# A graph layer and a routed feed-forward layer: one layer norm in place of two, self loops on GpSimd, groups handed over by tile, logits in two banks

## The reference

```python
def gnn(x, C2, A):                       # called with C2 = A = adj
    adj = (A + A.T) * 0.5
    adj = adj + eye(N)                   # the self loops
    dinv = where(deg > 0, sum(adj, 1) ** -0.5, 0)
    adj = dinv[:, None] * adj * dinv[None, :]
    return C2 @ adj @ x                  # computed as adj @ x = Z, then C2 @ Z = Y

x1 = x + gnn(layernorm(x), adj, adj)     # layernorm: (x - mean) / sqrt(var + 1e-5)
t = layernorm(x1)                        # first norm of x1
h = (t - mean(t)) / sqrt(var(t) + 1e-5) * gamma + beta    # second norm, inside the FFN
shared = silu(h @ q(sw1).T) @ q(sw2).T   # q: rows rounded to -1, 0, 1 times mean |w|
probs = softmax(h @ router_w.T); e = argmax(probs)        # 8 experts
out = x1 + shared + max(probs) * (silu(h @ q(w1[e]).T) @ q(w2[e]).T)
```

## Time and profile before

| | |
|---|---|
| median of 3 runs | 729.55 us (727.76 to 730.76) |
| the profiled execution | 729.79 us |
| its span, first to last instruction | 728.1 us |
| mean granted TensorE clock | 0.986 of full |
| busy: TensorE, its weight loads | 91%, 53% |
| busy: VectorE, ScalarE, GpSimd | 67%, 54%, 28% |
| DMA | 151.68 MB, 208 GB/s on average |

### The profile page before, as it was taken

How to read it: one execution, slowest core, us unless ns; L and a number is a source line. 1 busy time by engine, 2 the same in 40 slices (tenths; PEclk the granted TensorE clock), 3 DMA queues, 4 the chain that set the end, 5 groups by cost and what they waited for, 6 DMA issues and landing times.

```text
span 728.1 us, 16147 instructions
## 1 busy us (share of the span) xinstructions
PE 659.4 (91%) x5313; PEld 385.2 (53%) x5313; DVE 488.8 (67%) x1071; ACT 390.1 (54%) x726; POOL 202.4 (28%) x195
## 2 busy tenths in 40 slices
PE   0799998999998999999868788799999999999995
PEld 0344443444444554444424365477767676777763
DVE  4878966646674556589899868966775465555554
ACT  2667547859986765777547662223342233233331
POOL 2123310000000000077666606620020445344332
PEclk9999999999999999999998999999999999999999
DMA  8999942675887787667566785354248677677751
GB/s 350 416 420 417 417 172 58 193 185 144 228 243 243 256 271 269 234 207 226 173 240 215 226 228 147 92 164 105 86 59 203 147 211 186 179 191 176 174 148 34
DMA packets 107103, 151.68 MB, mean 208 GB/s; under 512 B 64286, under 2 KB 64286, under 8 KB 102944
## 3 DMA queue, kind: packets, MB, share of 16 engines
q1 hardware_dynamic: 91280, 117.74, 52.5%
q0 software_dynamic: 6960, 20.99, 9.7%
q10 hardware_dynamic: 8800, 12.09, 5.2%
HBM read 119.57 MB, written 19.16 MB: 191 GB/s over the span
## 4 chain that ended last, share of the span: by engine, by line
PE 60%; DVE 13%; DMA 10%; issue 7%; POOL 4%; ACT 4%; DVEq 0%; SPq 0%; ACTq 0%; POOLq 0%
PE bank L1536 14%; PE bank L1509 14%; PE bank L1375 9%; PE bank L1377 9%; PE bank L1376 9%; DMA region<-in_adj_t 5%; DMA work<-in_w 2%; PE bank L1414 2%; DVE work L1081 2%; POOL xb L578 2%; DVE xb L1127 1%; POOL xb L580 1%; ACT junk L732 1%; DVE s L1062 1%; DMA work<-in_adj_t 1%
## 5 line engine op out<-in xcount | busy, mean ns | idle before, releaser
L1536 PE MATMUL bank<-region,work 128*128 (+1 forms) x624 | 142.5, 382 | 4.2 <-DVE work L1229 4.2
L870 ACT ACTIVATE work<-work 128x512 f32<-128x512 f32 x78 | 48.5, 622 | 180.6 <-DVE work L1219 180.6
L1375 PE MATMUL bank<-zreg,work 128*128 (+1 forms) x256 | 98.2, 384 | 13.6 <-DVE work L1150 10.8
L1509 PE MATMUL bank<-zreg,region 128*128 128x128 f16 x1728 | 100.9, 219 | 0.0
L1509 PEld LDWEIGHTS bank<-zreg,region 128*128 (+1 forms) x1728 | 98.1, 98 | 4.3
L1376 PE MATMUL bank<-zreg,work 128*128 (+1 forms) x256 | 98.1, 383 | 0.0
L1377 PE MATMUL bank<-zreg,work 128*128 (+1 forms) x256 | 98.1, 383 | 0.0
L1536 PEld LDWEIGHTS bank<-region,work 128*128 128x128 f16 x624 | 59.2, 98 | 70.8 <-issue 8.9
L1375 PE MATMUL bank<-region,work 128*128 128x512 f16 (+1 forms) x192 | 74.8, 389 | 23.1 <-DVE region L994 23.1
L732 ACT ACTIVATE junk<-work 128x512 f16<-128x512 f32 x124 | 77.7, 626 | 22.8 <-DMA work<-in_w 20.7
L575 POOL TENSOR_TENSOR rb<-rb,power 128x2 f32<-128x2 f32 x16 | 17.4, 1087 | 255.5 <-DVE rb L1141 255.4
(11 more groups left out here) (158 smaller groups left out, 1009.8 us busy)
## 6 DMA issues: line engine op xcount, KB each, us to landing
work<-in_w SPq DMA_DIRECT2D x62, 512.0 KB, 4.1
region<-in_adj SPq DMA_DIRECT2D x16, 1024.0 KB, 10.8
region<-in_adj_t SPq DMA_DIRECT2D x16, 1024.0 KB, 7.5
work<-in_adj_t SPq DMA_DIRECT2D x32, 384.0 KB, 4.2
zreg<-s_scratch SPq DMA_DIRECT2D x24, 256.0 KB
xb<-in_w SPq DMA_DIRECT2D x10, 512.0 KB, 4.2
zreg<-in_x SPq DMA_DIRECT2D x4, 1024.0 KB, 9.8
h_scratch<-hb POOLq DMA_DIRECT2D x16, 256.0 KB, 3.7
```

Of the source, the lines that this page charges most:

```text
L870: nc.scalar.activation(h1[:, cols], pre[:, cols], ACT.Silu).then_inc(h1_ok, 1)
L1375: nc.tensor.matmul(dst, a_hi, b_hi, start=start, stop=False, skip_group_check=True)
L1509: last = nc.tensor.matmul(ps_h[b][f // 4][:, (f % 4) * P:(f % 4 + 1) * P], w, ht[n % RING][:, c:c + P], start=(f % 4 == 0 and d == 0 and h ...
L1536: last = nc.tensor.matmul(ps_y[b][:, :].rearrange("p (d c) -> p d c", d=DB), h1hl[:, b, h, f * P:(f + 1) * P], w, start=(f == 0 and h == 0 ...
```

## The change

Five edits come together.

1. The two norms of x1 become one. The mean of the first result is zero and its variance v/(v+eps), so both roots make one: 1/sqrt(v * (1 + eps) + eps * eps). VectorE takes the statistics of x1 once, GpSimd one power, and VectorE applies it as (x1 - mean) * gamma and then * root + beta, four scalar_tensor_tensor for a pair. The parts stand after steps 0 and 2 of a macro. GpSimd's multiply and add are gone; among the shared tiles the parts are placed anew.
2. The self loops are added to the matrix: GpSimd adds a diagonal of 2 to one 128x128 square per block, in `a_in` for blocks 0 to 7 and in `kept` for 8 to 15, behind `degree_root`. ScalarE waits for it (`diag_ok`). The 32 matmuls are gone. GpSimd's loop over the stream is written out.
3. `z_acc` counts tiles. The last step of a group counts up after each tile in place of its own step count, and ScalarE evicts tile by tile. The first step of the next group opens its banks itself and waits for each bank's eviction.
4. Group 2 of Z takes its banks in the order 4, 5, 0, 1, and the first step of Y takes the tiles of banks 2, 3, 4, 5, 0, 1 in that order.
5. The logits alternate between banks 7 and 6, and wait for the routing row of the tile before the last.

```diff
-Z_GROUPS = [..., (12, 4, (0, 1, 4, 5))]
+Z_GROUPS = [..., (12, 4, (4, 5, 0, 1))]
+        ps_lg = [bank[7], bank[6]]
@@ gpsimd
-fill=2.0 * A_SCALE
+fill=2.0
+            def add_identity(j):
+                i, s = divmod(j, UNROLL)
+                if j < Z_GROUPS[0][1]:
+                    pool.wait_ge(sum_ok, j + 1)
+                    square = a_in[:, s, j * P:(j + 1) * P]
+                else:
+                    pool.wait_ge(rest_ok, j + 1)
+                    g, c = divmod(j * P - G0_COLS, REST // 2)
+                    square = kept[:, g, j, c:c + P]
+                nc.gpsimd.tensor_tensor(square, square, ident2[:, :], ALU.add).then_inc(diag_ok, 1)
 ...
                     degree_root(UNROLL * i + s + 1, (s + 1) % 2)
+                    add_identity(UNROLL * i + s + 1)
 ...
-                for r in range(2):
-                    pool.wait_ge(ln_var, t + r + 1)
-                    nc.gpsimd.tensor_tensor(rb[:, :, 1], rb[:, :, 0], power[:, 0:2], ALU.pow).then_inc(ln_root, 1)
-                for b in range(2):
-                    pool.wait_ge(ln_normed, t + b + 1)
-                    nc.gpsimd.tensor_tensor(xb[:, b, :], xb[:, b, :], gb[:, 0, :], ALU.mult).then_inc(h_seq, 1)
-                    pool.wait_ge(h_seq, t + b + 1)
-                    nc.gpsimd.tensor_tensor(xb[:, b, :], xb[:, b, :], gb[:, 1, :], ALU.add).then_inc(h_ok, 1)
+                pool.wait_ge(ln_var, pair + 1)
+                nc.gpsimd.tensor_tensor(rb[:, :, 1], rb[:, :, 0], power[:, 0:2], ALU.pow).then_inc(ln_root, 1)
@@ scalar
+                if j < Z_GROUPS[0][1]:
+                    act.wait_ge(diag_ok, j + 1)
 ...
-                    act.wait_ge(rest_step, k - 3)
+                    act.wait_ge(rest_step, k - 3 - (k - 3 >= NT))
+                    if k - 3 == NT:
+                        act.wait_ge(z_acc, Z_GROUPS[2][0])
 ...
-                act.wait_ge(z_acc, g + 1)
                 for k in range(count):
+                    act.wait_ge(z_acc, t0 + k + 1)
@@ vector
-            NORM_STEPS = {0: (), 1: (0, 1, 2), 2: (0, 2, 3)}
+            NORM_STEPS = {0: (), 1: (0, 2), 2: (0, 2)}
 ...
+                    nc.vector.tensor_scalar(rb[:, :, 0], mvb[:, :, 1], 1.0 + EPS, EPS * EPS, ALU.mult,
+                                            ALU.add).then_inc(ln_var, 1)
 ...
+                dve.wait_ge(ln_root, pair + 1)
                 for b in range(2):
+                    nc.vector.scalar_tensor_tensor(out=xb[:, b, :], in0=x1[b], scalar=mvb[:, b, 0:1], in1=gb[:, 0, :],
+                                                   op0=ALU.subtract, op1=ALU.mult).then_inc(ln_normed, 1)
+                for b in range(2):
+                    dve.wait_ge(ln_normed, t + b + 1)
+                    nc.vector.scalar_tensor_tensor(out=xb[:, b, :], in0=xb[:, b, :], scalar=rb[:, b, 1:2],
+                                                   in1=gb[:, 1, :], op0=ALU.mult, op1=ALU.add).then_inc(h_ok, 1)
 ...
             shared_tile(0, 0, [], [(route, 0), (norm_parts, 0, 12)])
             turn_s2(2, 2 * CHUNKS)
             norm_parts(1, 12)
-            shared_tile(1, 1, [2], [(route, 1), (norm_parts, 2, 12)])
-            norm_parts(0, 14)
+            shared_tile(1, 1, [2], [(route, 1), (norm_parts, 0, 14)])
             shared_tile(2, 0, [4], [(route, 3), (norm_parts, 1, 14)])
-            shared_tile(3, 1, [6], [(route, 5), (norm_parts, 2, 14)])
+            shared_tile(3, 1, [6], [(route, 5)])
@@ tensor
+                    if last_one:
+                        last.then_inc(z_acc, 1)
+                if not last_one:
+                    last.then_inc(p1_step, 1)
 ...
+            EVICTED = {1: (1, 2, 3, 4), 2: (5, 6, 9, 10)}
 ...
+                        if opens:
+                            pe.wait_ge(zlo_ok, EVICTED[g][k])
 ...
+            Z_LAST = {bank: t0 + k + 1 for t0, count, banks in Z_GROUPS for k, bank in enumerate(banks)}
 ...
-                    for k in range(count):
-                        if first and s == 0 and g == 0 and k in Z_GROUPS[2][2]:
-                            pe.wait_ge(zlo_ok, 13 + Z_GROUPS[2][2].index(k))
+                    opens = first and s == 0 and g == 0
+                    for k in (2, 3, 4, 5, 0, 1) if opens else range(count):
+                        if opens:
+                            pe.wait_ge(zlo_ok, Z_LAST[k])
 ...
-                if n:
-                    pe.wait_ge(l_ok, n)
+                if n >= 2:
+                    pe.wait_ge(l_ok, n - 1)
+                lgs = ps_lg[n % 2]
```

101 lines of the change are left out of this document (40 added, 61 removed).

## The result

The changed kernel takes 702.64 us, the median of four runs (701.08 to 707.49), against 730.15 us for the kernel before in the same session; the ratio is 0.964, with a 95% interval of 0.9601 to 0.9679. Its profiled execution took 702.86 us with a span of 701.2. Forecast were 704.3 us and a range of 697 to 713. Run again beside other kernels, unchanged, it took 702.32 us (ratio 0.9625, 0.959 to 0.9661).

What follows compares the result with a forecast made beforehand. Five regimes bound it in turn: DMA, VectorE and TensorE nearly tied; TensorE with ScalarE; TensorE; VectorE; routing waits behind a norm. Gains 0.4 + 4.3 + 2.6 + 0.7 + 1.0 + 7.8 + 8.7 = 25.5 us gave 704.3, range 697 to 713.

Steps and rivals of the forecast that it cites:

- Part 1: Self loops in the adjacency stream: 32 matmuls go, 16 GpSimd adds come; gain 0.4 us, from a 2 loss to 1.2.
- Part 2: Handover from Z's first group to its second: eviction by tile removes TensorE's wait; gain 4.3 us, 3.3 at least.
- Part 3: Handover from Z's second group to its third: ScalarE decides and starts evicting sooner; gain 2.6 us, bounds 2.0 and 5.7.
- part 4: Handover from Z's last group to Y: TensorE begins with banks 2 and 3, long free; gain 0.7 us, 0 to 1.5.
- Part 5: Layer norm in Y's second and third groups: less VectorE and GpSimd work and contention; gains 1.0 and 7.8 us.
- Then come 15.1, 16.1 and 12.5 us: 43.7: Walk by step through macros 9 to 11 of Y's third group: 43.7 us in place of 51.5, gaining 7.8.
- rival (a): ScalarE or the weights' buffer loop bounds macros 8 to 11, the clock falls again; 710.5 us, chance 0.18.
- The greater part is contention: Layer norm: GpSimd stretches VectorE's instructions by 11 us from 375 to 427; multiplies and adds make three quarters.
- Part 6: Start of the shared tiles: two logits banks and the shorter norm remove waits for routing rows; gain 8.7 us, 5 to 9.5.
- Rival (c): Shared tiles: two banks don't free the logits, the row before being late behind the norm; 709 us, chance 0.10.
- The exclusion rule: Two-SBUF-input VectorE and SBUF-reading GpSimd instructions exclude each other; norm meeting subtractions would lose 13 us of VectorE (712).
- Rival (d): Adjacency stream: GpSimd adds wait out VectorE's two-input instructions, delaying each block; 744 us, deciding from 2.6 us per add, chance 0.03.

Runs made afterwards that it cites:

- half sums: Changed kernel with ScalarE summing the weights' absolute values over half of the columns in the third and fourth early round: 702.69 us, ratio 0.9599.
- by group: Changed kernel with ScalarE waiting for a whole group of Z before it evicts the first tile: 710.08 us, ratio 0.9678.
- two orders: Changed kernel with the x part's power ahead of the fourth block's self loop and shared tiles' loads after macros 9 and 10: 700.8 us, ratio 0.9613.
- low half first: Changed kernel with VectorE's low half ahead of the norm in Y's third group, x part's power ahead of the fourth self loop: 702.62 us, ratio 0.9614.
- one bank: Changed kernel with the logits in one bank, each set waiting for the row sum of the block before: 707.77 us, ratio 0.9662.

## Why the prediction was right, step by step

- **Part 1 (0.4).** Right in size: block 8 starts at 70.17 after 1.89 us of idle (forecast near 70.6), and the place behind the last plain matmul is reached 0.31 us earlier (112.58 instead of 112.89). But the sizes inside are not those of the forecast. The contention that it called the real cost, 0.4 us onto each L994, isn't there: that instruction (L1010 now) takes 0.75 us in all 16 blocks of both kernels, and block 11 starts at 85.72, 1.3 us earlier than before, not at 86.6. What was put at nothing took it back: block 12 waits 0.79 us, and 0.4 of that is the addition ahead of the x part's power, which I had taken up by the wait for DMA (without additions 0.39 is left). The additions last 0.6 us, not 0.4, since they wait out the end of the low half.
- **Part 2 (4.3).** Measured 4.28. One run gives 1.85 of it to ScalarE's count per tile; 2.4 are left for the rest.
- **Part 3 (2.6) and part 4 (0.7).** TensorE gained 4.0 us at the third group and gave 0.7 back at Y's start: 3.3 together, as forecast. ScalarE bounds it, as the half sums show. No run parts the new order of the banks (edit 4) from it. ScalarE's first high half came at 204.95, 6.5 us earlier, where my sum had 7.3: for 1.55 us it waited for a weight tile that had been issued 6.3 us before. A fall of the granted clock to 0.86 from 200 to 210 was not in the forecast.
- **Part 5 (8.8).** Measured 3.7 in Y's second group and 5.5 in the third, 9.2 together; I had 1.0 and 7.8. In the second group the two norms bring 2.1 to 3.1 of the 3.7 back (73.9 and 73.6 us in the two kernels that have them, 71.4 and 70.7 in the changed one); where the remainder is from, no run shows. In the third, 0.7 came in macro 8, and macros 9 to 11 take 46.6 us (47.1 in the second profile), not 43.7: 4.9 gained of 7.8, and on both sides of the 47 at which I called myself wrong. The failed step is "Then come 15.1, 16.1 and 12.5 us: 43.7": three waits of 1.3 to 1.5 us behind the norm and one of 2.8 on a turned weight chunk stayed, and with the first three removed others came. These waits fit rival (a)'s mechanism, and 2.9 of the 4.8 us that it took off this term.
- **"The greater part is contention ... the multiplies and adds make three quarters of it."** Too large. In the group it speaks of, the kernel with both on GpSimd loses 4.1 us and the one with a second norm 8.2: half, and part of that is the longer chain. Up to the product after shared tile 1 it is 4.9 against 20.3.
- **Part 6 (8.7).** Measured 9.5. But the sum tied it to the two banks as much as to the norm. The banks are worth 1.3 us. With the second norm back all of it is gone, and the 3.15 us wait for the power is back. Rival (c) was built on the banks and had no weight to carry.
- **The exclusion rule.** The norm's instructions with two inputs took 0.744 and 0.746 us on the mean of 16 each, as the one alone in the earlier trace rows, so the loss of 13 us that I had put beside the Trainium skill (SBUF — State Buffer, on engine ports) didn't come. In this kernel none of the 32 meets a subtraction. Beside the subtractions ran ternary instructions, and a pair of these took 2.50 us instead of 0.90; the one low half that began behind a subtraction, at 401.58, took 1.64 instead of 0.68. So the trace bears the rule out where the two meet, as it does for the additions above.
- **Rival (d).** It didn't come, by the reason that the prediction gave against it: an addition does wait out VectorE, but for one instruction and not for three of 1.22 us, and here mostly for the last 0.3 to 0.5 us of one of 0.75. Its threshold of 2.6 us per addition doesn't follow from its own sum either (4.7 us of work in 5.5 leave 0.8).

That the total came within 2 us of the forecast is partly luck: part 5's two halves were off by 2.7 and 2.3 us with opposite signs, and part 1 came out by a cost that wasn't there and one that was left out.

## What to carry to other kernels

Where a pass of statistics, a small power on another engine and a second pass stand in a chain, count the chain's length before the engines' busy time: here, with the order of the shared tiles, taking one link out was worth 15 us and moving the chain's wide operations off the slower engine 5. Hand an accumulator over tile by tile, on both sides of the handover. When four waits look alike and sit behind one instruction, moving it pays only if what stands behind the next one is ready, and a single profiled execution can't price a microsecond: compare the start of the same matmul and know the scatter of each stretch.

## What the runs showed of the hardware

- An instruction of VectorE with two inputs in SBUF and one of GpSimd that reads SBUF took turns by whole instructions in these traces. Of 56 additions of 128x128, 32 began inside such an instruction and ended 0.28 or 0.29 us after its end; 24 began outside and took 0.43. In the other direction low halves of 128x512 took 0.67 to 0.69 us, and 1.64 to 1.76 where they began in the first 0.4 us of a multiply, addition or subtraction of 128x512. So the price goes with what is left of the instruction that began first; a wide instruction of GpSimd can leave more of it than a narrow one. A mean over a group (1.03 us of 15) hides this.
- Some one-input instructions were stretched in the same way. The 128x2 instruction ahead of the ternary ones took 0.16 to 0.17 us, or 1.1 to 1.25, each time begun inside a 128x512 instruction of GpSimd: in Y's third group five of nine before, one of nine in the changed kernel, and one of nine with gamma and beta on GpSimd. Which instruction is hit is a matter of timing.
- The length of an idle time doesn't tell whether TensorE's granted clock falls. At the first second product of the shared tiles it stayed at full speed after 2.26 us (changed) and 2.48 us (by group), and fell to half after 2.06 (two orders), 2.15 (low half first) and 2.33 us (one bank). Each such fall cost about 1.7 us, in matmuls every 0.43 us. The difference between two runs of one stretch is often just such a fall.
